# Perceiver block on one core: context probabilities in one buffer, logits in pieces of 512, 512 and 64 columns

## What is computed

```python
def _L0_xattn_ref(x, latents, Wq, Wkv, Wo, ln1_w, ln1_b, ln2_w, ln2_b):   # x: (8, 1024, 256), latents: (8, 64, 256)
    xn = _layernorm(x, ln1_w, ln1_b)
    ln = _layernorm(latents, ln2_w, ln2_b)
    q = ln @ Wq
    kv = jnp.concatenate([xn, ln], axis=-2) @ Wkv
    k, v = jnp.split(kv, 2, axis=-1)
    q, k, v = (heads(q), heads(k), heads(v))            # 16 heads of 64
    logits = jnp.einsum('bhld,bhsd->bhls', q * scale, k * scale)
    w = jax.nn.softmax(logits, axis=-1)
    out = jnp.einsum('bhls,bhsd->bhld', w, v)
    out = out.transpose(0, 2, 1, 3).reshape(B, L, INNER)
    return out @ Wo
```

## Time and profile before

| | before |
|---|---|
| median of 3 runs | 920.51 us |
| profiled execution | 921.28 us |
| its span, first to last instruction | 919.6 us |
| TensorE busy, share of the span | 812.8 us, 88% |
| VectorE busy | 530.1 us, 58% |
| ScalarE busy | 385.0 us, 42% |
| GpSimd busy | 256.7 us, 28% |
| mean granted TensorE clock | 0.954 |

### The profile page before, as it was taken

The page is one execution under the profiler, slowest core; times in us unless marked ns, Lnnn a source line. Parts: engine busy times, 40 slices in busy tenths (PEclk is TensorE's granted clock), DMA queues, the critical chain, the costliest instruction groups (busy, mean ns, idle before and its releaser), DMA issues.

```text
span 919.6 us, 13716 instructions
## 1 busy us (share of the span) xinstructions
PE 812.8 (88%) x5443; PEld 699.2 (76%) x5443; DVE 530.1 (58%) x992; ACT 385.0 (42%) x888; POOL 256.7 (28%) x179
## 2 busy tenths in 40 slices
PE   5899999999999999999999999997636565788996
PEld 3589999999999999999999999984312232257885
DVE  5364565555555555556547453445899999971112
ACT  2444444443544443444444343432853434403341
POOL 3717008008005205303502600001245545610000
PEclk9999999999999999999999999997858989898998
DMA  8100100100100010010030100000200000061720
GB/s 297 46 1 1 47 1 2 46 2 1 42 6 1 6 42 1 1 47 1 2 115 1 10 1 1 1 1 2 92 0 0 0 1 0 0 240 37 273 92 25
DMA packets 22499, 34.21 MB, mean 37 GB/s; under 512 B 6488, under 2 KB 18336, under 8 KB 21408
## 3 DMA queue, kind: packets, MB, share of 16 engines
q1 hardware_dynamic: 22432, 33.29, 10.6%
HBM read 32.77 MB, written 0.52 MB: 36 GB/s over the span
## 4 chain that ended last, share of the span: by engine, by line
PE 76%; DVE 16%; issue 4%; DMA 1%; ACT 1%; SPq 0%; DVEq 0%; POOL 0%; POOLq 0%; ACTq 0%
PE psum L1155 21%; PE psum L1193 20%; DVE state L782 12%; PE psum L1176 6%; PE psum L1197 4%; PE psum L1128 3%; PE psum L1475 3%; PE psum L1465 3%; PE psum L1216 2%; PE psum L1111 2%; PE psum L1135 2%; PE psum L1226 2%; PE psum L1207 2%; PE psum L1288 1%; DMA wq_sb<-in_L_xattn_Wq_dram 1%
## 5 line engine op out<-in xcount | busy, mean ns | idle before, releaser
L901 ACT ACTIVATE pt_hi<-psum 128x512 fp32r<-128x512 f32 (+1 forms) x192 | 87.0, 488 | 268.6 <-PE psum L1176 169.8
L624 DVE TENSOR_TENSOR pt_lo<-psum,pt_hi 128x512 fp32r<-128x512 f32 (+1 forms) x192 | 100.3, 550 | 101.4 <-ACT pt_hi L901 101.2
L1193 PE MATMUL psum<-kvn_hi,pt_hi 128*128 128x256 f32 x512 | 149.6, 292 | 0.0
L1193 PE MATMUL psum<-kvn_lo,pt_hi 128*128 128x256 f32 x512 | 144.0, 281 | 0.0
L1193 PE MATMUL psum<-kvn_hi,pt_lo 128*128 128x256 f32 x512 | 143.8, 281 | 0.0
L632 DVE TENSOR_REDUCE rowmax<-psum 128x1 f32<-128x728 f32 x64 | 58.7, 918 | 110.0 <-PE psum L1155 110.0
L782 DVE TENSOR_TENSOR_SCAN state<-dec,drive 128x2048 f32<-128x2048 f32 x16 | 107.1, 6691 | 0.1
L1193 PEld LDWEIGHTS psum<-kvn_lo,pt_hi 128*128 128x128 f32 x512 | 97.3, 190 | 0.1
L1193 PEld LDWEIGHTS psum<-kvn_hi,pt_hi 128*128 128x128 f32 x512 | 97.1, 190 | 0.1
L1193 PEld LDWEIGHTS psum<-kvn_hi,pt_lo 128*128 128x128 f32 x512 | 97.1, 190 | 0.0
L1155 PE MATMUL psum<-kvt_hi,qk_hi 128*128 128x364 f32 (+1 forms) x384 | 90.7, 345 | 4.3 <-ACT prob L939 2.5
(11 more groups left out here) (216 smaller groups left out, 1471.0 us busy)
## 6 DMA issues: line engine op xcount, KB each, us to landing
w<-in_L_ffn_W_dram SPq DMA_DIRECT2D x16, 1024.0 KB, 7.5
ctx_nat<-in_ctx_dram SPq DMA_DIRECT2D x8, 1024.0 KB, 4.9
wk_nat<-in_L_xattn_Wkv_dram SPq DMA_DIRECT2D x1, 1024.0 KB, 6.5
wq_sb<-in_L_xattn_Wq_dram SPq DMA_DIRECT2D x1, 1024.0 KB, 11.7
wv<-in_L_xattn_Wkv_dram SPq DMA_DIRECT2D x1, 1024.0 KB, 13.9
wo<-in_L_xattn_Wo_dram SPq DMA_DIRECT2D x1, 1024.0 KB, 16.2
q_t<-in_L_attn_W_in_dram SPq DMA_DIRECT2D x1, 1024.0 KB, 7.4
x_lat<-in_x_dram SPq DMA_DIRECT2D x1, 512.0 KB, 3.7
```

Source lines behind the costliest of these rows:

```text
L624: dve.tensor_tensor(pt_lo[u][rows, t0:t1, :], where[rows, 0:(t1 - t0) * P].rearrange("p (t m) -> p t m", m=P), pt_hi[u][rows, t0:t1, :].bi ...
L901: act.activation(pt_hi[u][rows, t0:t1, :], where[rows, 0:(t1 - t0) * P].rearrange("p (t m) -> p t m", m=P), ACT.Copy)\
L1193: pe.matmul(PV, w[u][:, j, :], x_[slot][:, j, :], start=(j == 0 and w is pt_hi and x_ is kvn_hi), stop=False)
```

## The change

One buffer `prob` of 1024 columns holds the context probabilities of every step, in place of two that alternate. The own 64 columns get two small buffers `prob_own` that alternate. `CUT` becomes 512, so the pieces of the logits have 512, 512 and 64 columns: `LG_A` is two full banks, and `LG_B` 64 columns. The loops, waits and counts of instructions are as they were.

```diff
-        prob = [sb(att, f"prob{i}", [P, S + L]) for i in range(2)]
+        prob = sb(att, "prob", [P, S])
+        prob_own = [sb(att, f"prob_own{i}", [P, L]) for i in range(2)]
...
         TWO = psum[:, 0:2, :]
-        CUT = 364
-        LG_A, LG_B = psum[:, 0:2, 0:CUT], psum[:, 2, 0:S + L - 2 * CUT]
+        CUT = 512
+        LG_A, LG_B = psum[:, 0:2, :], psum[:, 2, 0:L]
...
-                    act.activation(prob[hp % 2][:, 0:2 * CUT].rearrange("p (a n) -> p a n", n=CUT), LG_A, ACT.Exp,
+                    act.activation(prob[:].rearrange("p (a n) -> p a n", n=CUT), LG_A, ACT.Exp,
                                    bias=nbias[slot][:, hp:hp + 1], scale=SCALE,
                                    accum_out=den_part[slot][:, hp, 0:1])
-                    act.activation(prob[hp % 2][:, 2 * CUT:], LG_B, ACT.Exp, bias=nbias[slot][:, hp:hp + 1],
+                    act.activation(prob_own[hp % 2][:], LG_B, ACT.Exp, bias=nbias[slot][:, hp:hp + 1],
                                    scale=SCALE, accum_out=den_part[slot][:, hp, 1:2]).then_inc(s_exp, 1)
...
-                        last = pe.transpose(TP[0][0:L, 0:P], prob[hp % 2][:, S:S + L], ident[:])
+                        last = pe.transpose(TP[0][0:L, 0:P], prob_own[hp % 2][:], ident[:])
                     else:
-                        last = pe.matmul(TP[0][half(slot), 0:P], prob[hp % 2][:, S:S + L], ident[:],
+                        last = pe.matmul(TP[0][half(slot), 0:P], prob_own[hp % 2][:], ident[:],
                                          start=True, stop=True)
...
-                                            prob[hp % 2][:, (4 * n + j) * P:(4 * n + j + 1) * P], ident[:])
+                                            prob[:, (4 * n + j) * P:(4 * n + j + 1) * P], ident[:])
```

## The result

The changed kernel takes 946.93 us (945.08 to 947.32, 4 runs) beside 920.35 us: a ratio of 1.0281, 95% interval [1.0261, 1.03]. That is 26.6 us slower where I had forecast 30.3 (950.8 us, range 942 to 957). The profiled execution is 947.22 us, its span 945.5 us against 919.6, with as many instructions as before, 13716.

A forecast was written before the change was run, and what follows sets the result against it. The attention was taken as bound by TensorE's matmul stream. A logits group of 2 x 234.4 + 110 = 579 ns against 500, over 384 groups, adds 30.3 us to the median of 920.5: 950.8 us, range 942 to 957.

The forecast's parts named there:

- What bounds the kernel: Attention: the stream of matmuls on TensorE, busy 70.00 of 70 us at full clock, so all 64 steps pay.
- The columns: Logits matmuls: 5.6 ns fixed and 0.447 ns a column, 234.4 ns for 512; by columns alone a group takes 503 ns.
- (2): Logits groups: wide matmuls save a fixed part, group 469 ns, 12 us less, time 908.6; chance 2%.
- (4): Logits: 512-column pieces at 213.3 ns with the load bound kept, group 537 ns, 14 us in all, time 935; chance 3%.
- The load behind the short piece: Logits: it starts with the 64-column piece and holds the next 512-column piece back for 110 ns, group 579 ns; 85%.
- Rival (1): Logits: that weight load is hidden or equal weights not reloaded, group 503 ns, 1.2 us in all, time 921.7; chance 6%.
- Rival (3): Logits: short piece and load in series, 613 ns, time 964, or load holding TensorE 188 ns, 657 ns, time 981; 4%.
- The last group of a step: End of a step's logits: the transpose's load costs the same 110 ns, so all six groups pay.
- Row maxima and exponentials: VectorE and ScalarE on the logits: 1443 ns as before and 1425 ns, hidden, less than 1 us in all, counted as nothing.
- One buffer: Context probabilities: no wait is added, and losing the second buffer costs nothing; moved addresses taken as 0.
- The range: Total time: low end 942, half way to 939 (512-column piece at 219 ns) with 1 us unpriced; high end 957, from 954.6.

The follow-up runs named there:

- the first experiment: The kernel before with pieces of 512, 512 and 64 columns, its two buffers for the probabilities kept: 948.66 us, ratio 1.03.

## Why the prediction was right, step by step

*What bounds the kernel.* Right. TensorE stays busy, and the 25.1 us by which the 64 steps are longer are all there at the end of the attention.

*The columns.* Right in kind and slightly high. Two pieces of 234.4 ns and 110 make 579 ns for a group; 575 was seen. That is 4 ns in each of 384 groups, 1.5 us. It is the sum of two errors that partly cancel, and so partly luck: in the logits a 512-column piece takes 230 ns and not the gather's 234.4, and the short piece with its load 115 and not 110. The rivals that priced wide pieces lower, (2) with a group of 469 ns and (4) with 537, fall with the 575.

*The load behind the short piece.* Right: about 110 ns, which makes a group some 75 ns longer under 64 columns, in the place that the forecast gave. Rival (1), hidden loads or loads spared for equal weights, falls by the 575 ns and by the two halves of 32 columns. Rival (3) falls as well: in series a group would be 613 ns, or 657, and with the 128-column piece it would be over 600, where 547 was seen.

*"The last group of a step is followed not by logits but by a transpose with 128 x 128 weights, whose load costs the same."* Wrong, and the larger part of the miss: this load left some 25 ns in the open where the others left 75, so the term was 50 ns x 64 = 3.2 us too large. The fault is a step earlier. I read the transposes' 109 ns as set by their load, because it was near the 112 ns of the two-column matmuls. But these loads are 140 ns long in the records and those of the logits 190. With a shorter load the 109 ns may come from something else about the transposes, which I did not test. The equality of two numbers was taken for one cause. The argument that load and columns aren't in series rested on this row; it held all the same, by the cuts at 480 and 440. The two terms together are 4.7 us, which taken from 30.3 leaves 25.6, and the 64 steps became 25.1 longer. That the times differ by 26.6, only 3.7 below the forecast, is the 0.7 us ahead of the first logits and the spread of the runs: the number came out about 1 us nearer than the mechanism.

*The range.* Its low end does not follow from its own words: half of the way from 950.8 to 939, less 1 us, is 943.9 and not 942. The measured 946.93 lies inside either.

The Trainium skill, "TensorE: Matmul & The Clock Gate", section "LDWEIGHTS (loading the stationary operand)", gives one rule for all loads, columns over 1.2 GHz, an estimate of 107 ns for 128. The fp32r loads come near it (some 110 ns more a group by the halves, 113 to 119 for a short piece and its load at the three widths). For the loads of the transposes the traces show less, by some 50 ns in the records and behind a short piece, and the measurement decides.

*Row maxima and exponentials.* Right. For 1024 and 64 columns VectorE takes 1224 and 215 ns where the straight line gave 1234 and 209, and ScalarE 1118 and 306 where it gave 1126 and 299:

```profile
L633 DVE TENSOR_REDUCE rowmax<-psum 128x1 f32<-128x1024 f32 x62 | 75.9, 1224 | 122.9 <-PE psum L1156 122.9
L634 DVE TENSOR_REDUCE rowmax<-psum 128x1 f32<-128x64 f32 x62 | 13.3, 215 | 0.0
```

```profile
L937 ACT ACTIVATE prob<-psum,nbias 128x1024 f32<-128x1024 f32 x62 | 69.3, 1118 | 11.8 <-DVE nbias L637 4.3
L940 ACT ACTIVATE prob_own<-psum,nbias 128x64 f32<-128x64 f32 x62 | 18.9, 306 | 0.0
```

*One buffer.* Right: nothing, by the first experiment and its trace. ScalarE writes `prob` after it has copied the turned tiles, as it did before, with 0.13 us between the two where it was 0.16:

```profile
314.54 1.09 ACT L902 ACTIVATE pt_hi<-psum 128x512 fp32r<-128x512 f32 x2 [2.93 <-PE psum L1177]
315.76 1.12 ACT L937 ACTIVATE prob<-psum,nbias 128x1024 f32<-128x1024 f32 x1
```

## What to carry to other kernels

When pieces of a moving operand are cut, cost each piece as the larger of its own columns and of the weight load of the matmul behind it: here 110 to 119 ns for fp32r weights of 128 columns, which a piece of 248 columns covered and one of 208 did not, so three even pieces had no load in the open and 512, 512 and 64 cost 2.8%. Count such a load for each matmul, also where three in a row have the same weights. And before two operations are given one price, compare their load records; the distance between starts alone hid here which of two causes set it.

## What the runs showed of the hardware that I had not expected

Weight loads of equal shape differ: 140 ns in the records for the transposes of `prob` and 190 for the fp32r matmuls of the logits, and behind a 64-column piece the first leaves about 25 ns in the open and the second 75. Matmuls over 64 rows between matmuls over 128 cost 0.54 us for three, where three over all rows, with zeros in half of them, cost 0.35, and 15 us in the whole kernel hung on it.
